# Four layers on one Trainium2 core: a second pair of banks for routed tiles, split down transform, moved router products and needs

## What is computed

```python
x = x + tanh(g_xattn[0]) * experts4(ln(x), token_ids, ctx)      # silu(h Wg) * (h Wu) Wd, 4 experts by token id
x = x + tanh(g_ffn[0])   * hadamard_mlp(ln(x))                  # fwht, 512 -> 2048 gated, fwht, 2048 -> 512
x = x + tanh(g_xattn[1]) * wkv(w, u, k=ln(x), v=ctx)            # a recurrence over 512 tokens of each batch
# last layer: 8 routed experts, top 2 of each token, and a shared expert
scores = softmax(xf @ gate_w); sel = top2(scores + bias)
out = silu(xf @ sw1) * (xf @ sw3) @ sw2                         # shared, hidden width 448
out = out.at[token].add((silu(r @ w1) * (r @ w3)) @ w2)         # routed, r = xf[token] * score
x = x + tanh(g_ffn[1]) * out
```

## Time and profile before

| what | value |
|---|---|
| median of 3 runs | 1278.4 us (1278.28 to 1281.13) |
| the profiled execution | 1271.4 us, span 1269.3 us, mean granted TensorE clock 0.986 |
| PE busy | 1210.6 us, 95% of the span |
| DVE, ACT, POOL busy | 52%, 35%, 36% |
| chain that ended last | 81% PE, 8% DVE, 3% issue, 3% ACT, 2% DMA |

### The profile page before, as it was taken

One profiled execution on the slowest core, in us unless ns is written; L12 is line 12 of the kernel. 1 busy time (PEld: TensorE's weight loads), 2 busy tenths in 40 slices (PEclk: granted clock), 3 DMA queues, 4 the chain that ended last, 5 costly groups with the idle time before them and its releaser, 6 DMA issues.

```text
span 1269.3 us, 17800 instructions
## 1 busy us (share of the span) xinstructions
PE 1210.6 (95%) x5789; PEld 1014.5 (80%) x5790; DVE 659.9 (52%) x1214; ACT 448.3 (35%) x754; POOL 458.2 (36%) x395
## 2 busy tenths in 40 slices
PE   3999989999999999999999988898999999999998
PEld 3788767787788878888788877787778888888887
DVE  7555358655446564656455657757623224333331
ACT  3333343333233523343245327564122222222222
POOL 2221023000022211321233414233766627986665
PEclk9999999999999999999999999998899999999999
DMA  7722158654759965794786503124553525645553
GB/s 246 290 83 67 54 204 329 251 198 187 276 184 323 337 226 197 261 360 177 242 310 240 182 1 116 34 87 164 226 183 121 203 83 172 218 147 176 174 160 128
DMA packets 64489, 241.75 MB, mean 190 GB/s; under 512 B 8428, under 2 KB 10696, under 8 KB 50728
## 3 DMA queue, kind: packets, MB, share of 16 engines
q1 hardware_dynamic: 41144, 155.93, 33.3%
q0 software_dynamic: 22816, 84.72, 20.4%
q10 hardware_dynamic: 464, 0.27, 0.1%
HBM read 165.13 MB, written 75.76 MB: 190 GB/s over the span
## 4 chain that ended last, share of the span: by engine, by line
PE 81%; DVE 8%; issue 3%; ACT 3%; DMA 2%; POOL 1%; SPq 0%; ACTq 0%; DVEq 0%; POOLq 0%
PE bank L1187 25%; PE bank L1354 18%; PE bank L1213 12%; PE bank L1387 9%; PE bank L1121 5%; PE bank L1143 4%; PE bank L1321 2%; PE bank L1372 1%; PE bank L1168 1%; PE bank L1158 1%; POOL xs_sorted L774 1%; DMA xs_sorted<-row,slw 1%; PE bank L1104 1%; PE bank L1131 1%; PE bank L1365 1%
## 5 line engine op out<-in xcount | busy, mean ns | idle before, releaser
L1187 PE MATMUL bank<-xTh,G 128*128 128x512 f32 x1024 | 275.0, 396 | 0.0
L1187 PEld LDWEIGHTS bank<-xTh,G 128*128 128x128 f32 x1024 | 190.8, 188 | 43.1 <-issue 5.3
L1354 PE MATMUL bank<-W,dxh 128*128 (+2 forms) x880 | 207.1, 378 | 11.1 <-DVE dmid L1813 8.2
L1354 PEld LDWEIGHTS bank<-W,dxh 128*128 128x128 f32 x880 | 164.5, 192 | 26.4 <-issue 11.2
L1213 PE MATMUL bank<-DN,bhh 128*128 128x512 f32 x512 | 157.9, 390 | 0.0
L1187 PE MATMUL bank<-xTl,G 128*128 128x512 f32 x512 | 137.1, 390 | 0.0
L1387 PE MATMUL bank<-W,dhh 128*128 (+1 forms) x440 | 127.3, 411 | 2.2 <-ACT dys L1026 2.1
L1671 DVE SCALAR_TENSOR_TENSOR bs<-bank,tab,bs 128x512 f32<-128x512 f32 x64 | 46.8, 731 | 147.1 <-PE bank L1187 147.1
L1811 DVE TENSOR_TENSOR dmid<-bank,dsg 128x384 f32<-128x384 f32 x55 | 30.5, 555 | 169.8 <-ACT dsg L1016 169.8
L1213 PEld LDWEIGHTS bank<-DN,bhh 128*128 128x128 f32 x512 | 96.2, 188 | 22.0 <-issue 2.4
L1187 PEld LDWEIGHTS bank<-xTl,G 128*128 128x128 f32 x512 | 96.1, 188 | 20.5
(11 more groups left out here) (273 smaller groups left out, 1947.8 us busy)
## 6 DMA issues: line engine op xcount, KB each, us to landing
G<-gate_up_split SPq DMA_DIRECT2D x48, 1024.0 KB, 7.5
DN<-down_split SPq DMA_DIRECT2D x24, 1024.0 KB, 4.9
gate_up_split<-G SPq DMA_DIRECT2D x16, 1024.0 KB, 6.9
wst<-in_L_ffn_w POOLq DMA_DIRECT2D x16, 896.0 KB, 5.5
y_all<-dys SPq DMA_DIRECT2D x55, 256.0 KB, 2.0
xs_sorted<-zero POOLq DMA_DIRECT2D x3, 3328.0 KB, 20.3
xsd<-xs_sorted SPq DMA_DIRECT2D x39, 256.0 KB, 3.2
down_split<-DN SPq DMA_DIRECT2D x8, 1024.0 KB, 4.1
```

The lines of the kernel that those rows point to most:

```text
L1187: mm = pe.matmul(bank[m][:, :], G[:, c % 2, f, h, m, i, :], a[b % 2][:, i, :], start=(n == 0), stop=(n == 3 * DC - 1))
L1354: mm = pe.matmul(bank[o][:, 0:width], a[par][:, k, :], w[:, bass.ds(slot, 1), at + k * step:at + k * step + width].rearrange("p a n -> p ( ...
```

## The change

Five edits, all in the order and the places of work; the outputs are computed from the same numbers.

1. Down transform in halves. From the fifth of the 16 down weights on (`HALVED = 4`), the full-precision product is replaced by two fp32r products, of the high part `wdp` (ACT, `prep_high`) and of the low part `wdq` (DVE, `prep_low`), both made one chunk ahead.
2. Router products of tiles 8 to 11 come a tile later, behind `d_up`, and the last-batch recurrence turns back in bank 7 instead of 5; the copies into `lg` are one copy.
3. The first shared tile waits for two of the four accumulators' reads instead of four; `d_down(0)` waits for the rest.
4. `needs()` is taken out of `results()` (tile 13) and runs at routed tile 20; POOL waits for it (`s_slot1`, 3) ahead of the first gather of results.
5. Routed tiles alternate between banks 2, 3 and banks 6, 7 (`up_banks`), and `d_up(t)` waits for `s_dmid` of two tiles before.

```diff
+        wdp = [place(f"wdp{i}", [P, D], WKV + (8 + 2 * i) * KB, F32R) for i in range(2)]
+        wdq = place("wdq", [P, FC, D], WD16, F32R)
+        signs = place("signs", [P, P], WKV + 12 * KB, F32R)
...
+        def up_banks(par, shared):
+            return (2, 3) if shared or par == 0 else (6, 7)
...
+            pool.wait_ge(s_slot1, 3)
             for t in range(TT):
                 n = pool.value_load(need_i[0:1, t:t + 1], min_val=1, max_val=NT1)
...
+            def prep_high(j):
+                for n in range(2 * j, 2 * j + 2):
+                    if n < HALVED + 2:
+                        act.wait_ge(s_bT, DC)
+                    else:
+                        act.wait_ge(s_pw, n - 1)
+                    act.activation(wdp[n % 2][:, :], wd16[:, n, :], ACT.Copy).then_inc(s_pwh, 1)
...
                     down_high(j + 1)
+                    if j == 0:
+                        act.activation(signs[:, :], cst[:, C_H:C_H + P], ACT.Copy).then_inc(s_pwh, 1)
+                    if j + 2 < NJ:
+                        prep_high(j + 2)
...
             def prep_w(j, f, bk):
-                pe.matmul(bank[bk][:, :], cst[:, C_H:C_H + P], wd16[:, 2 * j + f, :], start=True, stop=True).then_inc(s_pw, 1)
+                n = 2 * j + f
+                if n < HALVED:
+                    pe.matmul(bank[bk][:, :], cst[:, C_H:C_H + P], wd16[:, n, :], start=True, stop=True).then_inc(s_pw, 1)
+                else:
+                    pe.wait_ge(s_pwl, n - HALVED + 1)
+                    pe.matmul(bank[bk][:, :], signs[:, :], wdq[:, n, :], start=True, stop=False)
+                    pe.matmul(bank[bk][:, :], signs[:, :], wdp[n % 2][:, :], start=False, stop=True).then_inc(s_pw, 1)
...
-                wait(pe, s_dmid, t)
-                sides = ((2, W_1, G_W, G_W if shared and t < HELD else HID), (3, W_3, HID, HID))
+                gate_bank, up_bank = up_banks(par, shared)
+                wait(pe, s_dmid, t if shared or isinstance(t, int) and t == TT else t - 1)
+                sides = ((gate_bank, W_1, G_W, G_W if shared and t < HELD else HID), (up_bank, W_3, HID, HID))
...
                 if t == 0:
-                    pe.wait_ge(s_acc, 4 * NB)
+                    pe.wait_ge(s_acc, 4 * NB - 2)
                 d_up(t, t % 2, True)
+                if HELD - 4 < t <= HELD:
+                    d_router(t + 3)
...
-                    wait(pe, s_lr, t - (HELD - 4))
-                    c_back(s, 5)
+                    c_back(s, 7)
...
-                if HELD - 4 <= t < HELD:
-                    if t in BACK_T:
-                        pe.wait_ge(s_co, NU - DC + BACK_T.index(t) + 1)
-                    d_router(t + 4)
...
+            def prep_low(j):
+                for n in range(2 * j, 2 * j + 2):
+                    dve.wait_ge(s_pwh, n - HALVED + 2)
+                    dve.tensor_tensor(wdq[:, n, :], wd16[:, n, :], f32(wdp[n % 2][:, :]), ALU.subtract).then_inc(s_pwl, 1)
...
                     down_low(j + 1)
+                    if j + 2 < NJ:
+                        prep_low(j + 2)
...
-                if HELD - 4 < t <= HELD:
-                    r = t + 3
-                    dve.wait_ge(s_lp, r - HELD + 1)
-                    dve.tensor_copy(lg[:, r, :], bank[5][:, (r - HELD) * E1:(r - HELD + 1) * E1]).then_inc(s_lr, 1)
...
                 d_hid(t - 1)
+                if t == TT + 4:
+                    needs()
```

More of the change, by code:

```diff
@@ L30 @@
 NK = F0 // P
+HALVED = 4
 NG = NB * NK
@@ L286, in program @@
         s_pw = sem("s_pw")
+        s_pwh = sem("s_pwh")
+        s_pwl = sem("s_pwl")
         s_wdt = sem("s_wdt")
@@ L348, in program @@
         s_lg = sem("s_lg")
-        s_lr = sem("s_lr")
         s_gwhi = sem("s_gwhigh")
@@ L1015, in d_gate @@
                 wait(act, s_dmid, t)
-                act.activation(dsg[:, :], bank[2][:, 0:HID], ACT.Silu).then_inc(s_dsg, 1)
+                act.activation(dsg[:, :], bank[up_banks(t % 2, t < TT)[0]][:, 0:HID], ACT.Silu).then_inc(s_dsg, 1)
             def d_hid(t):
@@ L1458, in _ @@
             d_x(TT + 2, 0)
+            pe.wait_ge(s_co, NU)
             d_up(TT + 1, 1, False)
@@ L1493, in _ @@
             chain(last)
-            dve.tensor_tensor(mask[:, :, :], ge[:, 0:E0, :], ge[:, 1:E0 + 1, :], ALU.subtract).then_inc(s_mask0, 1)
-            dve.wait_ge(s_mask0, 1)
+            chain(dve.tensor_tensor(mask[:, :, :], ge[:, 0:E0, :], ge[:, 1:E0 + 1, :], ALU.subtract))
             flat = "p e i -> p (e i)"
@@ L1810, in d_mul @@
                 full = HF * P
-                dve.tensor_tensor(dmid[t % 2][:, 0:full], bank[3][:, 0:full], dsg[:, 0:full], ALU.mult)
+                ups = bank[up_banks(t % 2, t < TT)[1]]
+                dve.tensor_tensor(dmid[t % 2][:, 0:full], ups[:, 0:full], dsg[:, 0:full], ALU.mult)
                 dve.tensor_tensor(dmid[t % 2][:, full:].rearrange("p (a n) -> p a n", n=HR),
-                                  bank[3][:, full:HID].unsqueeze(1).broadcast_to([P, 2, HR]),
+                                  ups[:, full:HID].unsqueeze(1).broadcast_to([P, 2, HR]),
                                   dsg[:, full:].unsqueeze(1).broadcast_to([P, 2, HR]), ALU.mult).then_inc(s_dmid, 1)
@@ L1829, in scores @@
                 dve.wait_ge(s_lp, TT - HELD)
-                dve.tensor_copy(lg[:, HELD + 4:TT, :].rearrange("p i e -> p (i e)"), bank[5][:, 4 * E1:(TT - HELD) * E1]).then_inc(s_lr, 1)
-                dve.wait_ge(s_lr, 5)
+                chain(dve.tensor_copy(lg[:, HELD:TT, :].rearrange("p i e -> p (i e)"), bank[5][:, 0:(TT - HELD) * E1]))
                 dve.wait_ge(s_lg, HELD)
@@ L1912, in results, with needs @@
                 chain(dve.tensor_copy(order_i[:, :], order_f[:, :]))
+                chain(dve.tensor_tensor(tcmp1[:, :, :], cst[:, C_IOTA:C_IOTA + 48].unsqueeze(2).broadcast_to([P, 48, E1 - 1]),
+                                        tend1[:, 0:E1 - 1].unsqueeze(1).broadcast_to([P, 48, E1 - 1]), ALU.is_ge))
+                chain(dve.tensor_reduce(tex1[:, :], tcmp1[:, :, :], AX.X, ALU.add))
+                dve.tensor_copy(tex1_i[:, :], tex1[:, :]).then_inc(s_slot1, 1)
+            def needs():
                 n = E1 * TT
@@ L1923, in results @@
                 chain(dve.tensor_reduce(need_f[:, :], reach[:, :, :].rearrange("p e i -> p i e"), AX.X, ALU.max))
[L1924 to L1928 removed]
+                dve.tensor_copy(need_i[:, :], need_f[:, :]).then_inc(s_slot1, 1)
             rows_done = [0]
@@ L1961, in _ @@
                 if t in BACK_T:
-                    add_out(NU - DC + BACK_T.index(t), 5)
+                    add_out(NU - DC + BACK_T.index(t), 7)
                 if t in VALUE_T[:2]:
```

12 lines of the change are left out of this document (4 added, 8 removed).

## The result

The changed kernel takes 1262.8 us (median of four runs, 1260.6 to 1263.1); the kernel before, beside it, 1278.3 us. The ratio is 0.9886, 95% interval 0.9859 to 0.9914: 15.6 us faster, 1.1%. The forecast of 1264.4 us was 1.6 us too high. In two later sets of runs the kernel before took 1270.4 and 1269.7 us and the changed one 1252.9 and 1253.2 (ratios 0.986 and 0.9864); in a third set, in which the changed kernel itself was not run, the kernel before took 1278.3 again.

A forecast was written before the change was run, and what follows sets the result against it. PE was taken as the bound in batch 0 and routed tiles, late waits in shared tiles. -4.9 + 1.5 - 3.6 - 5.0 - 2.0 = -14.0 us, from median 1278.4 to 1264.4 us; range 1259 to 1271.5.

The forecast's parts named there:

- Part 1: Batch 0, down transform: 12 full-precision transforms of 0.86 us become two fp32r products, 0.455 us; -4.9 us, ends -3.5 and -4.9.
- the cover: Batch 0: added ACT copies and DVE subtractions, made one chunk (18 us) ahead, fit idle time; first chunk's 1.3 us slip absorbed.
- Part 2: First shared tile: starts 1.2 us earlier, but `c_keys` wait grows to about 2.5 us; gain 0, longer pause counted +1.5 us.
- a pause that chills more than one tile: Sign of being wrong: the pause at `c_keys` lowers the clock in more than one tile.
- Part 3: Tiles 5 to 8: `add_out` waits shrink, low clock goes, new `dmid` wait about 1.0 us; -3.6 us, ends -1.5 and -5.0.
- Part 4: Tile 15: without `needs`, `dmid` wait falls 2.3 us, low clock 2.7 us; -5.0 us, ends -1.9 and -5.5.
- my second rival: Tile 15: the rows' buffers take over from `needs` as the wait; gain there only 1.9 us, total 1267.5 us; chance 9%.
- Part 5: Tiles 17 and 18: waits for `dmid` of 1.26 and 0.80 us both go; -2.0 us taken, ends -1.2 and -2.1.
- the claim that the other tiles gain nothing: Routed loop: PE's stretch is 98% busy without waits, so two pairs of banks bring nothing to the other 37 tiles.
- The rule that spoke against the change: Tile 20: POOL's SBUF reads block DVE's two-SBUF-input instructions; two `needs` instructions caught cost some 6 us of DVE, nothing of PE.

## Why the prediction was right, and where it wasn't

**The total** was 1264.4 forecast, 1262.8 measured, inside the range. From the first profile of before to the second of the changed kernel, which has neither of the two losses, the span falls by 15.9 us (2.0 of them ahead of batch 0), from the second of before by 13.2; the sum was 14.0. Parts 1, 3 and 5 are confirmed in mechanism and within about 1 us in size, part 4 for its wait, part 2 in its sign in the traces:

| part | forecast | stages | by undoing it: trace, median |
|---|---|---|---|
| 1, halves | -4.9 | -5.0 | 5.0, 5.4 |
| 2, accumulators | +1.5 | +0.1 to +3.2 | -0.1 to -3.2, +2.6 |
| 3, router and bank 7 | -3.6 | -4.7 | 3.1, 6.1 |
| 4, needs | -5.0 | -4.9 | 2.1, 3.8 |
| 5, bank pairs | -2.0 | -2.2 | 2.3, 2.4 |

"Stages" compares the first profile of before with the second of the changed kernel, for parts 1 and 2 with the kernels in which they are undone. The medians of undoing add up to 20.3 us, more than the 16.5 to 17.5 us between the two kernels in the same sets, so a single one of them is good to a few us only.

**Part 1** holds to 0.1 us, the cover too.

**Part 2.** The wait grew to 2.56 us as forecast. The low clock behind it came as 3.03 us for eight matmuls in tile 1 (second profile, granted clock 0.65 from 753.98 to 758.90 us), and in two of three profiles of the changed kernel again in tile 3, behind 2.2 us of waiting for POOL's `cev`, which makes 41.0 us from tile 0 to 4. The upper end I gave, +1.5, was too narrow: it is +3.2. I had named a pause that chills more than one tile as a sign of being wrong; whether the pause at `cev`, and with it tile 3, is a consequence of part 2 was not tested.

**Part 3** was under-sized by about 1 us. The mechanism stands: no wait for `add_out`, no low clock, and the new wait for `dmid` at tile 8, 0.57 us where I said 1.0. I had left 0.5 and 0.8 us of waiting at tiles 5 and 6; there remain less than 0.2 and 0.51. The wait for `dxr` at tile 4, 1.52 us before, stays (1.61 and 1.78).

**Part 4** has the right sum for a partly wrong reason. I said the wait would be 0.3 to 0.5 us; it is 1.01 and behind it stand rows that DVE held back for their buffers (waits of 1.06 us for a scatter), a small share of my second rival. And the 2.7 us for the clock is no fixed price of this pause. This is what the clock did after nearly the same pause at the same place, tile 12, first and second profile of the changed kernel (granted clock 0.66 from 873.92 to 879.00, and 1.00 from 879.08 to 884.00):

```profile
873.92 3.17 PE L1388 MATMUL bank<-W,dxh 128*128 128x448 f32 x8 [3.32 <-DVE dmid L1856]
```

```profile
879.08 1.86 PE L1388 MATMUL bank<-W,dxh 128*128 128x448 f32 x8 [3.15 <-DVE dmid L1856]
```

A twin row that shows a slow group behind a pause shows what can happen, not what will. I took it as the price, and as an end of the range it would have been right.

**Part 5** holds, and so does the claim that the other tiles gain nothing.

**The rule that spoke against the change** was borne out. I wrote that two to five of the eight instructions of `needs` could be caught at tile 20, and that two of them would cost some 6 us of DVE and nothing of PE. First profile of the changed kernel, DVE and then POOL:

```profile
960.67 0.27 DVE L1967 CAST reach<-reach_i 128x128 f32<-128x128 int32 x1
960.97 1.86 DVE L1968 SCALAR_TENSOR_TENSOR reach<-tst,reach 128x128 f32<-128x128 f32 x1
962.86 4.67 DVE L1970 TENSOR_TENSOR reach<-reach,has 128x128 f32<-128x128 f32 x1
967.57 0.38 DVE L1971 TENSOR_REDUCE need_f<-reach 128x16 f32<-128x128 f32 x1
```

```profile
960.79 1.89 POOL L659 CAST W<-wst 128x2048 fp32r<-128x2048 f32 x1
962.76 4.62 POOL L664 TENSOR_TENSOR W<-wst,W 128x2048 fp32r<-128x2048 f32 x1
```

The two that read two tiles in SBUF took 1.86 and 4.67 us, each until POOL's instruction had ended. In the kernel before, at 911.80 and 912.13 us, they took 0.29 each; so the two cost DVE 5.95 us more. From tile 19 to 21 PE takes 17.8 to 18.0 us in the three profiles of the changed kernel, against 17.7 and 17.8 before.

**What the prediction lacked.** I priced that lock only where the change put work (tile 20). It was in the kernel already, under 16 additions with SP's loads behind them. At tile 36 it costs 3.8 to 4.4 us in five of the eight profiles of changed kernels with the old order of SP's loads; neither of the two profiles of before has this loss, so whether the kernel before pays it in other runs isn't shown. And I carried the sum of one profiled execution to the median without asking what the 7.0 us between the two were. In that set the profiles differ by 8.3 us and the medians by 15.6; that the median came within 1.6 us of the forecast was in part luck. It rests on both kernels moving by nearly the same amount between the sets (8 to 9 and 10 us).

**Still open** is the loss at tile 13: 7 to 9 us in every profile of changed kernels from two sets, none in the others, and none in either profile of before. It has the size of the step between the sets, and the first profile of before is 7 us below its median, so before may have it too in most of its runs; no trace shows it. What stops PE, ACT and DVE at once, while POOL goes on issuing its scatters, was not found. No packet of the queues that carry instructions falls between the starts of tiles 13 and 14 in any of the five profiles (in the first the nearest are at 874.8 and 904.6 us), so the traces show no late loading of code there.

## What to carry to other kernels

The waits that the prediction worked out came within some 0.7 us of what the profiles show; the low clock behind them did not, so it belongs in the range rather than in the sum. Where DVE reads two tiles in SBUF while POOL works, find the queue behind the buffer that DVE frees, and see whether the load that PE needs can stand ahead of the one that can be held; here it took the loss at tile 36 away, though the median didn't show it. When one profile stands apart from the median of its runs by more than the effect that you look for, take a second one, and compare stage lengths rather than spans.
